# A language-model tower on one core: half of the code-book gates by DRAM, blocks ordered unit first, 8-bit weights rounded in the first stage, projections unrolled in one stage

## The chip, the cores and the metric

One core of one Trainium2 chip runs the whole kernel in one launch. The metric is the device time of that core in microseconds (us). Its engines are TensorE (PE), VectorE (DVE), ScalarE (ACT), GpSimd (POOL) and SyncE (SP), which only issues DMAs here. The profile calls the weight loads of TensorE PEld.

## The reference, cut to what matters

2048 tokens (16 rows of 128) of width 192 pass an embedding and four layers; each layer adds an attention part and a feed-forward part, both behind a layer norm. Changed are the embedding, the norm ahead of the first feed-forward (16 experts, the best 8 of a router), the 8-bit attention of the third layer and its code-book feed-forward.

```python
# embedding
return token_emb + pos_emb[None, :, :] + segment_emb    # segment: rows of a 2-row table
# 8-bit attention, third layer
x_int, s_x = _act_quant(x)            # one scale: the largest |x| of all tokens
wq_int, s_wq = _weight_quant(w_qkv)   # a scale for each output row
acc_s = s_x * s_wq
qkv_int = jnp.einsum('bnc,oc->bno', x_int, wq_int) + _round_ste(b_qkv / acc_s)
qkv_f = qkv_int * acc_s
s_qkv = jnp.maximum(jnp.max(jnp.abs(qkv_f)) / QMAX, EPS)
...
out_int = jnp.einsum('bnc,oc->bno', ctx8, wp_int) + _round_ste(b_proj / out_s)
return out_int * out_s
# code-book feed-forward, third layer: S=8 subspaces, M=64 codes, K=4 kept, R=16, H=32
z = jnp.einsum('nd,sdr->nsr', xf, P)
scores = jnp.einsum('nsr,smr->nsm', z, C)
topv, topi = jax.lax.top_k(scores, K)
w = jax.nn.softmax(topv, axis=-1)
h = jax.nn.gelu(jnp.einsum('nsr,nskrh->nskh', z, W1[sidx, topi]) + b1[sidx, topi])
yl = jnp.einsum('nskh,nskhr->nskr', h, W2[sidx, topi]) + b2[sidx, topi]
comb = jnp.einsum('nskr,nsk->nsr', yl, w).reshape(N, S * R)
out = jax.nn.gelu(comb @ G1 + g1b) @ G2 + g2b
```

## The kernel before, in words

P is 128, D 192 and NB 16: a tile is 128 tokens, and four tiles (GS) make one of four groups (NG) of 512 columns (GT). Each part of the tower is one or more stages; a stage has one program for each engine, tied by semaphores, and ends with all engines at one point. Within a stage an engine takes its instructions in the order in which the code writes them. `Chain` (`c.step`) makes each step of VectorE wait for the one before it.

**First stage**, `embed_stage` (L95). SyncE loads the ids and small tables, GpSimd gathers 16 tiles of rows of the table by indirect DMA into `held_h`, all on one semaphore. VectorE waits for all of them, adds the positions to all 16 tiles in one instruction (L145), and then adds the segment row in 32 instructions (L149).

**Norms**, `norm_stage`. VectorE centres and scales tiles, PE turns them (L289 to L293), ScalarE copies the turned columns out. Only the norm of the first feed-forward has a `wide` output: of its upper 64 columns it wants two copies, in rows 0 to 63 and 64 to 127, so PE multiplies by the identity twice (L293), and one ScalarE copy takes the group. PE runs three groups of turns ahead, then multiplies the first one by the router matrix (L305); ScalarE keeps the logits (L323) and VectorE picks the best 8 (from L387).

**8-bit attention**, `s_l2attn`: the norm n4; `quant_weights_stage` (L2554, tiles `qw_`), which takes the largest |x| (L2611) and lets GpSimd share it over the partitions (L2581), meanwhile rounds the weights, turns them and makes a row of scales, then rounds x and makes the rows (the reciprocal is L2628); `quant_qkv_stage` (L2633, tiles `qq_`), which for each of 16 tiles copies x on GpSimd, turns it on PE, copies it on ScalarE, multiplies, and on VectorE adds the bias (L2700), multiplies by the scale row and takes the maximum; L2709 is the maximum over tiles. Then the heads, and `quant_out_stage` (L2962, tiles `qo_`), with three VectorE instructions a tile (L3048, L3051, L3054) in a loop over pairs of tiles.

**Code-book feed-forward**, `codes_stage` (L1319, tiles `cod_`). All 64 codes of each subspace are computed densely and weighted by gates that are zero but for the best four. A group's work is 32 steps. Step k takes block k % 16 (four codes of 32 hidden units, so 128 rows) of the four subspaces of half k // 16. One subspace of a step is a unit:
- PE: the up matmul into one of three `up` banks (L1459, waits until ScalarE has read what was in the bank), and a matmul of `sel_g` with the turned weights `wt` (L1464), which spreads the gates of the four codes over 128 rows into one of three `gate` banks (waits until VectorE has read what was there);
- ScalarE: gelu with the bias (L1588), into `hp`;
- VectorE: `hp` times the gate bank (L1721).

Behind the four units of step k PE does the down matmuls of step k - 1 (L1480, f32, for the four subspaces side by side) into `comb`; at the first step of each half they are preceded by the b2 bias matmuls (L1475, 24 of them).

Into these steps the order written out in the code puts the preparation of the next group: projection at k = 5, 6; scores at 7 to 10; VectorE's best-4 search at 8 to 11 (L1672, L1686); differences at 9 to 12; spread of z at 12 to 19; marks at 13 to 16; ScalarE's exponential at 15 (L1566); totals and the normed weights at 17 to 21, and their splitting into four bf16 parts `wp` at 19 to 25 (ScalarE's high and mid parts, VectorE's rest and low parts L1710, L1714); and eight turns of `wp` on PE with eight ScalarE copies into `wt` (L1538, 128 x 1024) at 24 to 31. The previous group's output is added at k = 2 to 4. A prologue does the same for the first group, with nothing beside it.

Elsewhere in the tower, and not changed: `b_scratch` in DRAM is read back by broadcast in the second layer (`mam_b_rows`), and the last layer's scatters are GpSimd's indirect DMAs (L1110) beside two VectorE instructions (L1224, L1225).

## Time and profile before

| what | value |
|---|---|
| the runs | 3571.7, 8737.26 and 3560.61 us; median 3571.7 |
| profiled execution | 3563.0 us, its span 3561.2 us |
| mean granted TensorE clock | 0.831 |
| PE busy | 2552.1 us, 72% |
| DVE busy | 2422.7 us, 68% |
| ACT busy | 1601.1 us, 45% |
| POOL busy | 838.6 us, 24% |
| DMA | 114.90 MB, 32 GB/s over the span |
| first stage | to 38.86 us |
| norm and router stage of the first feed-forward | some 236 to 300 us |
| rounding stage, projection stage (8-bit) | 1796.7 to 1823 us, 1824 to some 1871 us |
| output projection (8-bit) | to 2200.9 us |
| code-book stage | norm to 2225, prologue to 2291.2, loop to 2812.2 us |

The busy shares are means over stages that differ: what a stage is worth is read from its own rows. A row of the windows gives each engine's busy time in a stretch; a row of the timeline gives start, duration, engine and line, the tiles out and in, and in brackets how long the engine was idle before it and who ended that. Lines are those of the kernel before.

### The profile page before, as it was taken

What the parts mean: (1) busy time and instruction counts of PE and PEld (TensorE: products, weight loads), DVE (VectorE), ACT (ScalarE), POOL (GpSimd) and SP (SyncE); (2) the same over time, 40 slices, a digit from 0 to 9 for tenths busy, and PEclk for the clock granted to TensorE, in tenths of its full rate; (3) what the DMA queues carried; (4) which work ended last, traced back from release to release, by engine and by line L of the source; (5) the groups of instructions that cost most, each with busy time, mean ns of one, the idle gap of its engine ahead of it and who ended that gap; (6) DMA issues with size and microseconds to landing.
All of it is one profiled execution on the core that took longest, in us unless ns stands there. A gap on an engine that the chain in (4) does not pass through costs nothing. (4 is left out here: it accounts for less than half of the span.)

```text
span 3561.2 us, 39662 instructions
## 1 busy us (share of the span) xinstructions
PE 2552.1 (72%) x13085; PEld 1555.3 (44%) x13132; DVE 2422.7 (68%) x5748; ACT 1601.1 (45%) x2888; POOL 838.6 (24%) x446
## 2 busy tenths in 40 slices
PE   3968995788888876699831112789889777776357
PEld 3955663333434333489721111323222266665335
DVE  4454335399999997211388997687787689999531
ACT  1111112566666652111116772677777545555211
POOL 1000000477676772267300000000000001111022
PEclk9767997799999997799955555899999889887668
DMA  1121001101010100511100000100000100000131
GB/s 37 19 80 45 1 1 31 63 33 70 26 63 33 58 37 0 159 43 40 51 10 1 1 1 1 56 1 1 1 1 1 53 23 1 1 1 1 58 134 54
DMA packets 61429, 114.90 MB, mean 32 GB/s; under 512 B 32685, under 2 KB 50188, under 8 KB 55884
## 3 DMA queue, kind: packets, MB, share of 16 engines
q1 hardware_dynamic: 55084, 100.16, 8.3%
q0 software_dynamic: 6144, 12.25, 1.1%
q8 instruction: 104, 1.70, 0.2%
q14 instruction: 97, 0.79, 0.1%
HBM read 98.31 MB, written 21.99 MB: 34 GB/s over the span
## 5 line engine op out<-in xcount | busy, mean ns | idle before, releaser
L1943 POOL TENSOR_TENSOR mam_st<-mam_du,mam_b_rows 128x1536 f32<-128x1536 f32 x128 | 439.5, 3440 | 172.8 <-PE mam_ysum L2012 172.3
L2173 DVE TENSOR_TENSOR_SCAN mam_st<-mam_da,mam_st 128x512 f32<-128x512 f32 x384 | 441.1, 1204 | 35.9 <-ACT mam_da L2113 18.2
L1721 DVE TENSOR_TENSOR cod_hp<-cod_hp,cod_gate 128x512 f32<-128x512 f32 x512 | 324.0, 681 | 122.2 <-ACT cod_hp L1588 122.0
L2012 PE MATMUL mam_ysum<-mam_st,held_ident 128*128 128x512 f32 x768 | 390.0, 648 | 2.2 <-DVE mam_st L2179 2.2
L1588 ACT ACTIVATE cod_hp<-cod_up,cod_b 128x512 f32<-128x512 f32 x512 | 318.8, 692 | 130.2 <-PE cod_up L1459 129.8
L2113 ACT ACTIVATE mam_da<-mam_delta,mamw_decay 128x508 f32<-128x508 f32 x384 | 254.2, 683 | 184.2 <-DVE mam_st L2173 149.5
L2294 POOL TENSOR_TENSOR att_probs<-att_se,att_neg 128x1536 f32<-128x1536 f32 x16 | 55.0, 3438 | 997.0 <-DVE att_neg L2499 997.0
L2179 DVE TENSOR_TENSOR mam_st<-mam_st,mam_c_ps 128x1536 f32<-128x1536 f32 x128 | 224.4, 1753 | 16.9 <-PE mam_c_ps L2007 13.4
L2012 PEld LDWEIGHTS mam_ysum<-mam_st,held_ident 128*128 128x128 f32 x768 | 159.8, 208 | 167.9 <-issue 160.8
L489 DVE SCALAR_TENSOR_TENSOR held_h<-x_dn,held_gate,held_h 128x192 f32<-128x192 f32 x256 | 89.1, 410 | 183.6 <-PE x_dn L456 181.9
L1464 PE MATMUL cod_gate<-cod_wt,cod_sel_g 128*128 128x512 bf16 x465 | 182.2, 392 | 39.0 <-DVE cod_hp L1721 38.4
L1459 PE MATMUL cod_up<-cod_zr,cod_w1r 96*128 96x512 bf16 x512 | 199.0, 389 | 14.1 <-ACT cod_hp L1588 9.5
L2499 DVE MATCH_REPLACE8 att_neg<-att_top,att_neg 128x128 f32<-128x128 f32 x768 | 201.1, 275 | 0.9 <-issue 0.9
L2492 DVE MAX8 att_top<-att_neg 128x8 f32<-128x128 f32 x768 | 154.8, 277 | 21.3 <-ACT att_neg L2412 14.2
L289 PE MATMUL n_turned<-held_ident,held_xw 128*96 128x128 f32 x224 | 46.2, 390 | 149.8 <-DVE held_xw L254 149.8
L479 ACT ACTIVATE x_ht<-x_up 128x512 f32<-128x512 f32 x96 | 52.1, 595 | 212.6 <-PE x_up L446 212.6
L1927 POOL MEMSET mam_u_pre<- 128x1608 f32 x1 | 1.4, 1437 | 607.6 <-POOLq L73 607.6
L1480 PE MATMUL cod_comb<-cod_hp,cod_w 128*16 128x512 f32 x1024 | 137.1, 608 | 3.0 <-DVE cod_hp L1721 3.0
L456 PEld LDWEIGHTS x_dn<-x1w_w,x_ht 128*128 128x128 f32 x768 | 123.5, 190 | 35.6 <-issue 35.6
L456 PE MATMUL x_dn<-x1w_w,x_ht 128*128 128x192 f32 x768 | 137.4, 333 | 0.0
L790 DVE TENSOR_TENSOR gr_o<-gr_dn,gr_w2c 128x192 f32<-128x192 f32 x40 | 14.3, 358 | 173.1 <-PE gr_dn L671 173.1
L722 ACT ACTIVATE gr_ht<-gr_up 128x512 f32<-128x512 f32 x80 | 39.2, 490 | 205.9 <-PE gr_up L660 205.9
(525 smaller groups left out, 5477.0 us busy)
## 6 DMA issues: line engine op xcount, KB each, us to landing
mam_b_rows<-b_scratch SPq DMA_DIRECT2D x32, 1024.0 KB, 8.0
slot_scratch<-in_slot_fresh SPq DMA_DIRECT2D x2, 3860.0 KB
sw_w<-in_L_w SPq DMA_DIRECT2D x1, 6144.0 KB, 18.6
gr_w<-in_L_w SPq DMA_DIRECT2D x1, 5376.0 KB, 42.2
gr_w<-in_L_w SPq DMA_DIRECT2D x1, 4608.0 KB
sw_w<-in_L_w SPq DMA_DIRECT2D x1, 4608.0 KB, 31.3
gr_rows<-slot_scratch SPq DMA_DIRECT2D x40, 96.5 KB, 1.9
x1w_w<-in_L_w SPq DMA_DIRECT2D x1, 3072.0 KB
```

The costliest lines, as they stand in the source:

```text
L456: last = nc.tensor.matmul(dn[x % 2][:, t, 0:D], ht[(g * NT + f) % NHT][:, t * P:(t + 1) * P], w2_sb[:, f, :], start=(f == first[e]), stop= ...
L1459: nc.tensor.matmul(up[u % BANKS][:], w1r[:, sub, f * P:(f + 1) * P], zr[g % 2][:, sub, :], start=True, stop=True).then_inc(up_ready, 1)
L1464: nc.tensor.matmul(gate[u % BANKS][:], sel_g[:, code, :], wt[g % 2][:, 2 * sub + half, :], start=True, stop=True).then_inc(gate_ready, 1)
L1588: nc.scalar.activation(hp[step % HOLD][:, j, :], up[u % BANKS][:], ACT.Gelu_apprx_tanh, bias=b1[:, sub * HT + f:sub * HT + f + 1]).then_in ...
L1721: nc.vector.tensor_tensor(at, at, gate[u % BANKS][:], ALU.mult).then_inc(gated, 1)
L1943: nc.gpsimd.tensor_tensor(st[it % N_ST][:], du[r % 2][:], along(b_rows[:, p % RING, n % PIECE, :], 1, [P, MC, MT]), ALU.mult)\
L2012: last = nc.tensor.matmul(ysum[:, c, :], m.ident[:], st[it % N_ST][:, c, :], start=False, stop=(it % DS == DS - 1))
L2113: nc.scalar.activation(live(da[:, c, :], r % 2), live(delta[r % 2][:, c, :], r % 2), ACT.Exp, scale=decay[:, c, n:n + 1]).then_inc(exp_rea ...
L2173: nc.vector.tensor_tensor_scan(fs, fa, fs, 0.0, ALU.mult, ALU.add).then_inc(scanned, 1)
L2179: nc.vector.tensor_tensor(x[:], x[:], along(c_ps[:], 1, [P, MC, MT]), ALU.mult).then_inc(weighted, 1)
L2492: last = nc.vector.max(top[:, n, :], cut[:, n, :])
L2499: last = nc.vector.match_replace(rev, top[:, n, :], rev, -BIG)
```

## The change

**Gates.** Of the four subspaces of a half, two (QP = 2) keep their gates from PE; for the other two (QD = 2) PE turns the normed weights themselves in f32 (`turn_gates`, k = 23, 24), ScalarE copies them to `turned_gates`, SyncE stores them to `gate_scratch` in DRAM by four DMAs a group (at k = 28), and for each step brings 512 KB back, broadcast over the hidden units (128 x 4 KB), into a ring of five `wide_gates`. The product of these subspaces reads SBUF. `up` has four banks, `gate` two. `wp` and `wt` hold only half, so that the splits go over 256 columns and four turns (k = 25 to 28) stand for eight. The rows of a block are ordered unit first, code second. The b2 bias of the two subspaces by DRAM is one f32 matmul each.

**8-bit attention.** The weights are rounded, turned and given their row of scales in the first stage, and stored in DRAM; n4 loads them ahead. The two stages become one, unrolled over the 16 tiles: x is rounded in four pieces, three accumulator banks, no GpSimd copies, the maximum is taken over tiles for each column, once a group, and multiplied by the scale row once at the end. The output projection is unrolled, its VectorE instructions take four tiles.

**First stage.** Positions and segments are summed into `base` while the gathers run (16 VectorE instructions, 16 ScalarE scaled copies, one sum), and each group of four tiles is added when its rows are in.

**Norm with `wide`.** One turn in place of two matmuls, and three ScalarE copies for one.

```diff
@@ embed_stage @@
+            sp.wait_ge(q_kept, 2)
+            sp.dma_start(m.q_turned, q_turned[:]).then_inc(q_out, 16)
+            sp.dma_start(m.q_row, q_row[:]).then_inc(q_out, 16)
+            sp.wait_ge(q_out, 32)
...
-            v.wait_ge(rows_in, 16 * NB)
-            c.step(nc.vector.tensor_tensor(m.h[:], m.h[:], along(pos[:], 1, [P, NB, D]), ALU.add))
...
+            c.step(nc.vector.tensor_tensor(base[:], base[:], second[:], ALU.add))
+            for g in range(NG):
+                at = slice(g * GS, (g + 1) * GS)
+                v.wait_ge(rows_in[g], 16 * GS)
+                last = nc.vector.tensor_tensor(m.h[:, at], m.h[:, at], base[:, at], ALU.add)
@@ norm_stage @@
-                        for row in (0, D - P):
-                            last = nc.tensor.matmul(bank[row:row + D - P, 1, at], x[:, P:D], m.ident[:], start=True,
-                                                    stop=True)
+                        last = nc.tensor.transpose(bank[0:D - P, 1, at], x[:, P:D], m.ident[:])
@@ codes_stage @@
-BANKS = 3
+BANKS = 4
+GBANKS = 2
+QP = 2
+GRING = 5
+SEND_AT = 28
...
+            def bring_gates(g, k):
+                step = g * STEPS + k
+                if step >= GRING:
+                    sp.wait_ge(gated, QS * (step - GRING + 1))
+                sp.dma_start(wide_gates[:, step % GRING].rearrange("p j t -> p (j t)"),
+                             along(m.gate_scratch[g % 2, k // HT, k % HT].rearrange("e j t -> e (j t)"), 0,
+                                   [SH, ET, QD * GT])).then_inc(gates_in[step % GRING], 16)
...
+                if j >= QP:
+                    return
+                if u >= QS:
+                    pe.wait_ge(gated, u - QS + 1)
...
+                    for j in range(QD):
+                        rows, at = slice(j * SM, (j + 1) * SM), 32 * (QP + j)
+                        nc.tensor.matmul(comb[at:at + 32, :], b2d[rows, half, :], turned_gates[rows, half, :],
+                                         start=True, stop=False)
...
-                v.wait_ge(gate_ready, u + 1)
-                nc.vector.tensor_tensor(at, at, gate[u % BANKS][:], ALU.mult).then_inc(gated, 1)
+                if j < QP:
+                    v.wait_ge(gate_ready, QP * step + j + 1)
+                    by = gate[j][:]
+                else:
+                    v.wait_ge(gates_in[step % GRING], 16 * (step // GRING + 1))
+                    by = wide_gates[:, step % GRING, j - QP, :]
+                nc.vector.tensor_tensor(at, at, by, ALU.mult).then_inc(gated, 1)
@@ quant_qkv_stage @@
-                    c.step(nc.vector.tensor_tensor(real[k][:], row, z.acc_row[:], ALU.mult))
-                    nc.vector.tensor_reduce(tile_max[:, bass.ds(t, 1)], real[k][:], AX.X, ALU.max,
-                                            apply_absolute_value=True).then_inc(dve2, 1)
+                if t % GS == GS - 1:
+                    g = t // GS
+                    c.step(nc.vector.tensor_reduce(parts[:, g], z.qkv[:, g * GS:t + 1].rearrange("p t n -> p n t"), AX.X,
+                                                   ALU.max, apply_absolute_value=True))
```

## Rows read from the trace of the kernel before

**Rows 1.** Windows, code-book loop: window, length, busy by engine, PEclk, DMA share, GB/s
```profile
2431.20:2570.80 139.60, 124.60 (x673) 40.01 (x684) 108.45 (x260) 103.18 (x167) 0.00 (x0) 0.96 0.00 1
...
2707.70:2812.20 104.50, 97.06 (x543) 28.28 (x550) 78.09 (x126) 76.00 (x127) 0.00 (x0) 1.00 0.00 1
...
2349.60:2353.60 4.00, 3.68 (x19) 1.20 (x19) 4.00 (x21) 3.02 (x7) 0.00 (x0) 1.00 0.00 0
```

**Rows 2.** Timeline, plain step: start, duration, instruction, [idle before, releaser]
```profile
2782.99 0.39 PE L1459 MATMUL cod_up<-cod_zr,cod_w1r 96*128 96x512 bf16 x1
...
2783.21 0.38 PE L1464 MATMUL cod_gate<-cod_wt,cod_sel_g 128*128 128x512 bf16 x1
...
2783.41 2.42 ACT L1588 ACTIVATE cod_hp<-cod_up,cod_b 128x512 f32<-128x512 f32 x4 [0.78 <-PE cod_up L1459]
...
2784.14 2.48 DVE L1721 TENSOR_TENSOR cod_hp<-cod_hp,cod_gate 128x512 f32<-128x512 f32 x4 [0.72 <-ACT cod_hp L1588]
...
2784.88 0.39 PE L1464 MATMUL cod_gate<-cod_wt,cod_sel_g 128*128 128x512 bf16 x1 [0.19 <-DVE cod_hp L1721]
...
2785.20 1.05 PE L1480 MATMUL cod_comb<-cod_hp,cod_w 128*16 128x512 f32 x8
...
2786.18 0.39 PE L1459 MATMUL cod_up<-cod_zr,cod_w1r 96*128 96x512 bf16 x1
```

**Rows 3.** Groups of instructions, code-book loop: busy, mean ns, idle before
```profile
L1538 ACT ACTIVATE cod_wt<-cod_misc 128x1024 bf16<-128x1024 bf16 x24 | 24.8, 1035 | 0.0
...
L1475 PE MATMUL cod_comb<-cod_wt,cod_b_part 128*32 128x512 bf16 x192 | 11.8, 381 | 0.0
...
L1714 DVE TENSOR_TENSOR cod_wp<-cod_ex,cod_wp 128x512 bf16<-128x512 f32 x12 | 8.2, 686 | 0.3 <-ACT cod_wp L1574 0.3
```

**Rows 4.** Timeline of DVE at the exponential of the first group
```profile
2362.70 1.28 DVE L1721 TENSOR_TENSOR cod_hp<-cod_hp,cod_gate 128x512 f32<-128x512 f32 x2 [4.14 <-ACT cod_hp L1588]
```

**Rows 5.** DMA view: GB/s in 40 slices of 200 us; one issue
```profile
GB/s 0 80 423 342 0 0 0 0 0 0 3 0 0 0 0 0 0 0 0 0 0 2 203 421 226 0 0 0 0 0 0 0 0 0 0 0 10 351 429 59
...
gr_w<-in_L_w SPq DMA_DIRECT2D x1, 5376.0 KB, 42.2
```

**Rows 6.** Timeline of the 8-bit projections, both stages
```profile
1796.69 3.35 DVE L2611 TENSOR_REDUCE qw_x_max<-held_xw 128x1 f32<-128x3072 f32 x1 [3.51 <-PEq L73]
...
1804.28 0.38 POOL L2581 PARTITION_ALL_REDUCE qw_x_all<-qw_x_max  x1 [72.60 <-issue]
...
1818.04 3.75 DVE L2628 RECIPROCAL qw_inv_row<-quant_acc_row 128x576 f32<-128x576 f32 x1
...
1863.73 0.75 DVE L2700 TENSOR_TENSOR quant_qkv<-qq_acc,quant_bias_row 128x576 f32 x1
...
1866.30 0.17 DVE L2709 TENSOR_REDUCE qq_all_max<-qq_tile_max 128x1 f32<-128x16 f32 x1
```

**Rows 7.** Timeline of the 8-bit output projection, first and last of 48
```profile
2179.04 0.36 DVE L3048 TENSOR_TENSOR qo_part<-qo_acc,qo_b_int 128x192 f32<-128x192 f32 x1 [0.21 <-DVE qo_b_int L3042]
...
2200.49 0.36 DVE L3054 TENSOR_TENSOR held_h<-held_h,qo_part 128x192 f32 x1 [0.15 <-DVE qo_part L3051]
```

**Rows 8.** Timeline of the first stage, VectorE
```profile
24.46 3.36 DVE L145 TENSOR_TENSOR held_h<-held_h,emb_pos 128x3072 f32<-128x3072 f32 x1 [17.99 <-DMA held_h<-in_table,emb_ids]
...
28.11 10.75 DVE L149 SCALAR_TENSOR_TENSOR held_h<-emb_types,emb_seg_is,held_h 128x192 f32<-128x192 f32 x32
```

**Rows 9.** Timeline of the last stage's scatters
```profile
3405.84 3.36 DVE L1225 TENSOR_TENSOR held_h<-held_h,sw_wide 128x3072 f32<-128x3072 f32 x1
3406.94 3.09 POOL L1110 DMA_INDIRECT slot_scratch<-held_xw,sw_slot_in  x1 [0.30 <-issue]
3410.33 0.96 POOL L1110 DMA_INDIRECT slot_scratch<-held_xw,sw_slot_in  x1 [0.31 <-issue]
```

**Rows 10.** Router stage of the first feed-forward: PE group, then a VectorE row
```profile
L293 PE MATMUL n_turned<-held_ident,held_xw 128*64 128x128 f32 x64 | 11.2, 449 | 0.0
...
271.87 0.29 DVE L387 TENSOR_REDUCE n_top_v<-held_logits 128x8 f32<-128x128 f32 x1 [10.82 <-ACT held_logits L323]
```

More of the change, by code:

```diff
@@ L1418, in spread_z, with turn_gates, turn_w @@
                 last.then_inc(ready, 1)
-            def turn_w(g, i, bank, ready):
-                t, h = i // 2, i % 2
+            def turn_gates(g, half, bank, ready):
+                pe.wait_ge(weighted, GS * (g + 1))
+                for t in range(GS):
+                    at = t * SS + half * QS + QP
+                    last = nc.tensor.transpose(bank[:, t * P:(t + 1) * P],
+                                               ex[:, at:at + QD, :].rearrange("p n e -> p (n e)"), m.ident[:])
+                last.then_inc(ready, 1)
+            def turn_w(g, t, bank, ready):
                 pe.wait_ge(w_low, GS * g + t + 1)
@@ new lines, in products @@
+            def products(t):
+                pe.wait_ge(copied, t + 1)
+                if t >= NACC:
+                    pe.wait_ge(summed, t - NACC + 1)
+                for n in range(2):
+                    for c in range(2):
+                        last = nc.tensor.matmul(acc[t % NACC][:, n, 0:N], xt[t % 2][:, c, :],
+                                                z.wt[:, c, n * N:(n + 1) * N], start=(c == 0), stop=(c == 1))
+                last.then_inc(acc_ready, 1)
+            pe.wait_ge(z.w_in, 48)
```

471 lines of the change are left out of this document (247 added, 224 removed).

## The prediction

> **What bounds the kernel now.** I read the windows first, to find out which of the changed stages are long. The code-book loop (first product to last) fills some 518 us of the 3561.2 us span: 139.6 us for the second group of four tiles, some 137 each for the first and third, 104.5 for the last [rows 1]. No engine is full there: in the second group PE 124.6, DVE 108.5 and ACT 103.2 of 139.6. So I opened the timeline of one step without side work [rows 2]. The reader is to see a ring: up product at 2782.99 (the next matmul 0.22 us later), four gelus from 2783.41, four products from 2784.14, the last gate matmul at 2784.88 (it had to wait for DVE to free one of three banks), then the down products from 2785.20, next step's first up product at 2786.18. Period 3.20 us, while four gelus take 2.31 (2.42 less the last one's tail: 0.58 each), four products 2.40 (0.60 each), and PE would need 8 x 0.22 + 1.0 = 2.8. Nearly all steps of the last group are of this kind. In steps that prepare the next group, DVE is the bound: at 2349.6 to 2353.6 it is busy 4.00 of 4.00 us [rows 1].
>
> **The loop, part by part.** Gates for two of four subspaces leave PE: 4 x 0.22 = 0.9 us a step less. Up banks go from 3 to 4, and a gate bank now waits only for the product one step back, so the ring no longer closes inside one step. What is left in a plain step: PE 6 x 0.22 + 1.0 + 0.1 = 2.4, DVE 2.40, ACT 2.31. The new ring spans two steps: a step's last product, down (0.06 + 0.99), up (0.43), gelu (0.69), four products (2.48), 4.7 us for two, 2.35 for one. I take 2.45, between 2.35 and today's 3.20. The product with the broadcast gate reads two SBUF operands in place of PSUM and one; a 512-column DVE instruction with SBUF operands takes 686 ns [rows 3] against 681, so no change in price. The last group has 27 plain steps and 5 with more (two b2 steps, three with the previous group's output): 27 x 2.45 + 2 x 5.0 + 4.3 + 2 x 3.2 = 87 against 104.5 + 3 for its first turns; gain 20.
>
> In the other groups I take each step as the largest of its three engines' sums and list what it loses. Steps 8 to 19 remain DVE's (products 2.4 plus up to 2.9 of maxima, marks, weights) and lose nothing. Steps 20 to 24: the four rest and four low instructions go over half the columns, 686 ns [rows 3] to about 0.36: 2.6 us. Steps 24 to 28: four turn copies of 1.03 us on ACT instead of eight [rows 3], 3.65 becomes 3.4: 1.4. Steps 29 to 31 become plain: 3.5. Steps 5 and 6 keep 1.9 us of projection on PE: 5.0 becomes 4.3: 1.4. Steps 7, 8 and 12: 1.7. Steps 1 to 4, the previous group's output: 2.1. The exponential stalls DVE for 4.14 us [rows 4]; with four banks ACT can be about one step ahead, so some 2.5 of stall is left, and a slow step less behind it: 3.1. Against that stand two gate copies of 0.58 on ACT and, at both halves, 12 bf16 bias matmuls two abreast instead of 24 four abreast (eight such batches are 11.8 us, 1.48 each [rows 3]; the same number of rounds stays) and two f32 ones (0.6 to 0.9), which the down products queue behind: 2.5. Sum 13.3 for each of three groups, to about 124. The whole loop: 3 x 13.3 + 20 = **60**. Bounds: 25 if plain steps fall only to 2.9 and others not at all, 78 if all overlaps fully.
>
> **The new transfers.** Each step brings 512 KB: 128 descriptors of 4 KB. SyncE issues it when the product five steps before is done, so it has some four steps, 10 us. The nearest row: the Mamba stage's broadcasts from scratch, of the same shape of source (1024 KB each), move 423 and 421 GB/s in full slices of 5 us [rows 5]. At that rate 512 KB is 1.25 us of a 2.45 us step. SyncE has nothing else in this stage but the four stores of the next group's gates at step 28, before the next group's first load, which has four steps of cover. Cost nil; without this cover each microsecond above 2.45 is paid in plain steps.
>
> **The stage's start.** Four wide turn copies of 1.03 [rows 3] fewer, and half of the splitting, less two gate copies: **4**, between 2 and 7. Its first transfer waits for the gate copies, is ready some 7 us later, and the first product that reads it is about 9 us away: hidden.
>
> **Projections.** Before, the weights' rounding and the 16 projections are two stages. From the maximum of x at 1796.69 to the maximum over all tiles at 1866.30 it is 69.6 us [rows 6]. New: x maximum 3.35; then GpSimd's all-reduce, which started at 1804.28 though its input was there at 1800.04 [rows 6]. This 4.2 us lay under the weights' work; now that is gone and DVE waits, to 1804.7 (1804.28 + 0.38). Scale steps 1.2, rounding in four pieces 12 x 0.5 = 6.0 (both estimates by width), rows with the 3.75 us reciprocal [rows 6] 5.6: 1817.5. Then 16 additions of 0.75 [rows 6] (0.82 with their waits) and four maxima over 2304 elements, 2.5 each (3072 elements take 3.35 [rows 6]): 23. Final maximum 2.5 + 0.8 + 0.8. That is 1844.8, where 1866.4 stands: **21**, bounds 14 (PE's matmuls, by an estimate 1.1 us a tile at half clock, become the pace) and 25 (the all-reduce comes at once). The multiply by the scale row and the maximum of each tile go; GpSimd's copies too, none of which ended a wait of DVE.
>
> **Output projection.** 48 small instructions of about 0.36 us, each with a gap behind it [rows 7], run from 2179.04 to 2200.85. New: 12 of 768 columns, 0.95 each: 11.4, after a rounding that four pieces make 0.9 longer: end 2191.0: **10**, bounds 6 and 12.
>
> **First stage.** The position add and 32 type adds, 14.4 us after the last row landed [rows 8], become one add of 3.36 ahead, and four of 0.9 as rows come in. ScalarE's part decides when the base is whole: weights' rounding on DVE ends at 12.5, PE turns and row matmuls to 17.8, copies to 18.7, 16 scaled copies of 0.25 (an estimate, between 0 and a 512-wide copy's 0.58) to 23, base whole at 26.4. SyncE's two stores end before. Now a stall: while DVE ran a 3.36 us instruction with two SBUF operands, a GpSimd indirect transfer took 3.09 us, in place of 0.96 beside an idle DVE [rows 9]. Gathers today run beside an idle DVE; new, DVE has some 13 us of such work then. At the same share the last row lands near 32, the stage's work ends near 33 instead of 38.86: **6**, bounds 2 and 10.
> The Trainium skill, page "SBUF — State Buffer", section "Who interferes with whom", has VectorE and GpSimd share a port pair that is held for a whole instruction; it counts the fast modes of tensor_scalar and copies among those that hold back GpSimd's descriptors, and infers that a tensor_tensor does not. The tensor_tensor of rows 9 does, so the measurement decides here; by the page only some 2 us of DVE's work would count and the term would be 8.
>
> **Router stage of the first feed-forward.** Each tile's two 64-row f32 matmuls are 64 matmul records of 449 ns [rows 10], and become one transpose: PE's turn of four tiles from 4.1 to about 1.9. The gate's first instruction comes at 271.87, 10.82 us late, for logits; the turn and route matmuls ahead of them run without a gap; three turns lie ahead of them: 3 x 2.2 = 6.6, less 0.3 for three ScalarE copies in place of one: **6**, bounds 0 (copies of 0.6 x 3 pace it) and 7.
>
> **Sum.** 60 + 4 + 21 + 10 + 6 + 6 = 107 from the profiled execution's 3563.0 (span 3561.2 and 1.8 around it): 3456. The runs shown are 3560.6 and 3571.7 (a third, 8737, is no measure); I name **3456**.
>
> **Rivals.** (A) PE stays the pace. For: PE is busy 97.06 of 104.5 us of the last group [rows 1] and is in order, with gate, down and bias matmuls in one queue. Then plain steps stay at 2.9, and prepared steps as they are: loop gain 25, time 3491. Against: its own sum is 2.4. (B) Slower than before: the broadcast is the pace. A 5376 KB load landed in 42.2 us, 128 GB/s [rows 5]. At 128 GB/s a step is 4.1 us, today's average, so there the loop gains nothing; the kernel is slower from (512 + 47) / 128 = 4.4 us a transfer on, and at 5.0 it takes 3563 - 47 + 128 = 3644. For: 64 MB are added to 115. Against: the two full slices at 421 to 423, with the same shape of source. (C) Transfers take 3.0 a step: plain steps alone pay, 39 x 0.55 = 21: 3477. (D) The new gates don't ease the loop, since steps 8 to 24 are DVE's and these rule: that is in the sum, and caps it; with plain steps gaining only in the last group the loop gives 35, time 3481.
>
> **Chances.** Forecast 0.66; A 0.12, B 0.05, C 0.07, D 0.10. The range 3415 to 3500 takes in A, C and D; B is left out, and what is better than 78 in the loop. About 2% can be told from no change, 71 us: faster 0.88, same 0.08, slower 0.04.
>
> **What would show it.** Plain steps of the last group at 2.4 to 2.5 us with DVE without gaps; groups near 124; the product's waits on a gates_in DMA at none; 3 us gathers in the first stage beside DVE's instructions; an idle DVE of about 4.5 us ahead of the projection's scale steps; 48 us from the maximum of x to that of all tiles. Wrong if a DMA ends DVE's waits, if steps 25 to 31 stay above 3.5, or if the granted clock in the loop falls below the 0.96 to 1.00 of now [rows 1].

## The result, and the profile after

The changed kernel takes 3469.99 us (median of 4 runs, 3465.39 to 3473.44), the kernel before 3569.11; the ratio is 0.9728, interval 0.9716 to 0.974, without the run of 8737.26 us of the kernel before. The profiled execution took 3465.39 us with a span of 3463.6, 97.6 us less than that of before. Forecast were 3456 us for the kernel and a gain of 107 us. Where the 97.6 us are, each stage from its first VectorE instruction to the next one's in the two timelines:

| stretch | before | after | gained | forecast |
|---|---|---|---|---|
| first stage | 39.9 | 33.0 | 6.8 | 6 |
| norm and retention (same code) | 197.9 | 192.9 | 5.0 | 0 |
| router stage and experts | 362.0 | 351.7 | 10.3 | 6 |
| projections, up to the heads | 75.8 | 63.8 | 12.0 | 21 |
| output projection | 36.3 | 29.2 | 7.1 | 10 |
| norm n5 and prologue, to the first product | 92.3 | 90.8 | 1.5 | 4 |
| code-book loop, first product to next norm | 526.8 | 466.9 | 59.9 | 60 |
| all else (same code, but for what n4 loads) | | | -5.0 | 0 |

These are two single executions. Four profiles whose loop has the code of the changed kernel (this one and three of the experiments) have it at 465.8 to 468.4 us, two with the code of before at 526.8 and 529.1: the 59.9 us are good to some 2 us, and a difference of 1 or 2 us between two profiles says nothing.

The windows of the loop's second and last group, against [rows 1]:

```profile
2376.70:2502.10 125.40, 107.24 (x571) 34.32 (x580) 105.36 (x261) 98.77 (x165) 0.00 (x0) 0.96 0.44 140
2627.20:2712.10 84.90, 81.27 (x467) 22.36 (x472) 75.95 (x127) 75.39 (x127) 0.00 (x0) 1.00 0.52 173
```

139.6 became 125.4 and 104.5 became 84.9. PE lost 17.4 us of busy time in the second group (124.6 to 107.2); the granted clock of these two windows is as before. New is the DMA column: in the last group 0.52 of the engines and 173 GB/s. That is 173 x 84.9 = 14.7 MB, 28 transfers of 524 KB, and 0.52 x 84.9 / 28 = 1.58 us of the DMA engines' time for each, of a step of 2.40. The timeline of two plain steps of the last group and of the first step of its second half, against [rows 2]:

```profile
2668.52 1.28 DVE L1850 TENSOR_TENSOR cod_hp<-cod_hp,cod_gate 128x512 f32<-128x512 f32 x2
...
2668.66 1.05 PE L1596 MATMUL cod_comb<-cod_hp,cod_w 128*16 128x512 f32 x8
...
2669.71 1.29 DVE L1850 TENSOR_TENSOR cod_hp<-cod_hp,cod_wide_gates 128x512 f32<-128x512 f32 x2
...
2670.92 1.28 DVE L1850 TENSOR_TENSOR cod_hp<-cod_hp,cod_gate 128x512 f32<-128x512 f32 x2
...
2671.06 1.05 PE L1596 MATMUL cod_comb<-cod_hp,cod_w 128*16 128x512 f32 x8
...
2673.62 0.60 ACT L1700 ACTIVATE cod_comb_t<-cod_comb 128x512 f32<-128x512 f32 x1
...
2674.27 1.47 PE L1587 MATMUL cod_comb<-cod_wt,cod_b_part 128*32 128x512 bf16 x12 [0.75 <-ACT cod_comb_t L1700]
...
2675.67 1.05 PE L1591 MATMUL cod_comb<-cod_turned_gates,cod_b2d 64*32 64x512 f32 x4
...
2676.65 1.05 PE L1596 MATMUL cod_comb<-cod_hp,cod_w 128*16 128x512 f32 x8
...
2678.78 1.29 DVE L1850 TENSOR_TENSOR cod_hp<-cod_hp,cod_gate 128x512 f32<-128x512 f32 x2 [2.66 <-ACT cod_hp L1708]
```

Down products stand at 2668.66 and 2671.06: a step is 2.40 us, where before it was 3.20. VectorE's products (two by PE's gates at 2668.52, two by the wide gates at 2669.71, then 2670.92) have no bracket, so it never waits: 4 x 0.60 is the step. Further down stands what I had priced too low. From 2673.62 ScalarE copies the sum, PE waits 0.75 us for it, then runs 12 bf16 bias matmuls (1.47), the f32 ones (0.98 to the next start), and only then the down and up products; VectorE is idle for 2.66 us, and from 2671.06 to 2676.65 this step takes 5.59.

The granted clock is not as before in the other groups. The whole loop, before and after, and an up matmul of step 11 of the second group after:

```profile
2294.00:2812.20 518.20, 465.04 (x2552) 146.58 (x2598) 404.54 (x908) 387.06 (x626) 0.00 (x0) 0.98 0.00 1
...
2254.20:2712.10 457.90, 404.01 (x2167) 124.18 (x2206) 392.42 (x908) 372.37 (x620) 0.00 (x0) 0.96 0.46 149
```

```profile
2424.17 0.63 PE L1569 MATMUL cod_up<-cod_zr,cod_w1r 96*128 96x512 bf16 x1
```

By groups it was 0.97, 0.96, 0.99 and 1.00 and is 0.94, 0.96, 0.95 and 1.00. At the lower of the two levels (0.5, 1.2 GHz) such a matmul takes 0.63 us and not 0.38, and step 11 of the second group, which stands in such a stretch, takes 5.84 us, where the first group's takes 4.02 at the full level. Before, this step took 4.01 in all three groups. In the four profiles of the new loop 31 to 38 us of it stood at the lower level, in the two of the old loop 17 and 21 us. TensorE has less to do in the new loop; that this is the reason is not shown.

Who waited for the wide gates, and how long their transfers took, from the view of that tile:

```profile
  ACT cod_hp L1708: 24.7, 34
...
DMA to landing us min/median/max: 3.4/3.9/7.6
```

In the loop VectorE waited for ScalarE before these products, never for a transfer; the slowest landed 7.6 us after its issue.

The projections, against [rows 6]:

```profile
1777.26 3.35 DVE L2748 TENSOR_REDUCE qq_x_max<-held_xw 128x1 f32<-128x3072 f32 x1 [4.37 <-PEq L73]
1783.04 0.38 POOL L2704 PARTITION_ALL_REDUCE qq_x_all<-qq_x_max  x1 [71.66 <-issue]
...
1793.00 3.75 DVE L2757 RECIPROCAL qq_inv_row<-quant_acc_row 128x576 f32<-128x576 f32 x1
...
1798.08 3.47 DVE L2762 TENSOR_TENSOR quant_qkv<-qq_acc,quant_bias_row 128x576 f32<-128x576 f32 x4
...
1801.70 4.20 DVE L2768 TENSOR_REDUCE qq_parts<-quant_qkv 128x576 f32<-128x2304 f32 x1 [0.15 <-DVE quant_qkv L2762]
...
1829.44 4.05 DVE L2770 TENSOR_REDUCE qq_most<-qq_parts 128x576 f32<-128x2304 f32 x1
```

From the maximum of x to the end of the maximum over the tiles (1835.07) it is 57.8 us, not 48. The first addition, at 1798.08, stands 20.8 us after the start as forecast, but by luck: the all-reduce came 1.8 us earlier than forecast (VectorE idle for 2.84 us and not some 4.5), and the rounding in four pieces took 7.8 us instead of 6.0. Behind it each maximum over a group takes 4.20 and the last 4.05, where I had 2.5, and the 16 additions with their gaps take 14.6, where I had 13.1.

The output projection's first and last instruction on VectorE, against [rows 7]:

```profile
2150.04 0.96 DVE L3110 TENSOR_TENSOR qo_work<-qo_acc,qo_b_int 128x768 f32<-128x768 f32 x1
...
2161.04 0.96 DVE L3113 TENSOR_TENSOR held_h<-held_h,qo_work 128x768 f32<-128x768 f32 x1
```

The first stage, against [rows 8]:

```profile
17.26 2.99 POOL L141 DMA_INDIRECT held_h<-in_table,emb_ids  x1 [0.31 <-issue]
...
19.25 5.62 ACT L179 ACTIVATE emb_second<-emb_types,emb_seg_is 128x192 f32<-128x192 f32 x16
...
24.98 3.36 DVE L207 TENSOR_TENSOR emb_base<-emb_base,emb_second 128x3072 f32<-128x3072 f32 x1 [5.55 <-ACT emb_second L179]
25.56 3.60 POOL L141 DMA_INDIRECT held_h<-in_table,emb_ids  x1 [0.30 <-issue]
```

VectorE waits for ScalarE's 16 scaled copies, 0.35 us each, then sums the base. One gather beside VectorE's instructions took 2.99 us and one 3.60.

The router stage, against [rows 10]: a group, then VectorE's first instruction of the gate.

```profile
L353 PE MATMUL n_turned<-held_ident,held_xw 128*64 128x128 f32 x16 | 6.1, 389 | 0.0
```

```profile
250.53 0.29 DVE L450 TENSOR_REDUCE n_top_v<-held_logits 128x8 f32<-128x128 f32 x1 [2.72 <-ACT held_logits L382]
```

The 64 records of 449 ns are 16 of 389, and the wait of 10.82 us is 2.72. The first 16 route matmuls of the stage, 258.71 in the timeline of before and 242.38 in that of after:

```profile
258.71 4.37 PE L305 MATMUL n_route_ps<-n_wr,x1w_wide 128*128 128x16 f32 x16
```

```profile
242.38 2.66 PE L364 MATMUL n_route_ps<-n_wr,x1w_wide 128*128 128x16 f32 x16
```

The granted clock also differs by chance. The retention stage between the first norm and the second has the same code in both kernels. Its window before, after, and in the second experiment below, which has the same code up to there as the changed kernel:

```profile
70.83:237.71 166.88, 149.65 (x1208) 137.93 (x1208) 77.05 (x167) 27.48 (x95) 0.00 (x0) 0.77 0.13 20
```

```profile
63.07:225.91 162.84, 146.43 (x1208) 134.91 (x1208) 77.20 (x166) 27.37 (x95) 0.00 (x0) 0.79 0.13 20
```

```profile
64.17:233.03 168.86, 152.41 (x1208) 140.21 (x1208) 77.18 (x166) 27.43 (x95) 0.00 (x0) 0.76 0.13 20
```

With 0.77, 0.79 and 0.76 granted it took 166.9, 162.8 and 168.9 us. Over all executions profiled here this stretch lay between 162.8 and 169.5 us, so its 4.0 of the 5.0 us in the table are no gain of the change. The other stretches moved 5.0 us the other way together, none by much more than 2, so the two cancel and the sum stands on the changed stages.

### The profile page after: what moved, and what is told of

It is laid out like the page before. It is cut to its first block and busy times, and to the rows that moved or that the text cites. A ratio compares the mean times of both kernels' runs of the same rounds, so it can differ in the third digit from the quotient of the medians.

```text
span 3463.6 us, 38446 instructions
## 1 busy us (share of the span) xinstructions
PE 2484.2 (72%) x12628; PEld 1541.3 (44%) x12668; DVE 2402.1 (69%) x5684; ACT 1594.3 (46%) x2912; POOL 830.5 (24%) x414
## 5 line engine op out<-in xcount | busy, mean ns | idle before, releaser
L1850 DVE TENSOR_TENSOR cod_hp<-cod_hp,cod_gate 128x512 f32<-128x512 f32 x256 | 163.5, 679 | 46.5 <-ACT cod_hp L1708 45.9
L1569 PE MATMUL cod_up<-cod_zr,cod_w1r 96*128 96x512 bf16 x512 | 180.1, 390 | 15.6 <-ACT cod_hp L1708 9.4
L1850 DVE TENSOR_TENSOR cod_hp<-cod_hp,cod_wide_gates 128x512 f32<-128x512 f32 x256 | 164.8, 685 | 24.8 <-ACT cod_hp L1708 24.7
L853 DVE TENSOR_TENSOR gr_o<-gr_dn,gr_w2c 128x192 f32<-128x192 f32 x40 | 14.3, 358 | 172.9 <-PE gr_dn L734 172.9
```

The lines of the kernel that those rows point to most:

```text
L1569: nc.tensor.matmul(up[u % BANKS][:], w1r[:, sub, f * P:(f + 1) * P], zr[g % 2][:, sub, :], start=True, stop=True).then_inc(up_ready, 1)
L1850: nc.vector.tensor_tensor(at, at, by, ALU.mult).then_inc(gated, 1)
```

## The experiments

**One half of the change each.** The first kernel is that of before with the code-book stage's edits alone (its constants, its units, the order of the rows of its weights), the second is the changed kernel with the code-book stage of before.

> The kernel before with the code-book part of the change alone. If the parts add up, as the sum of the prediction has it, this stage gives what the traces of before and after show between its first VectorE instruction and the next norm: 586.4 - 523.3 = 63 us, so about 3563 - 63 + 1 = 3501 us, ratio 0.982 to 0.984. Rival: the transfers or the clock couple it to its neighbours, then the sum with the other half of the change misses 98 us by more than 5.

Measured: 3504.26 us, ratio 0.9827 (0.9811 to 0.9843). The loop took 465.8 us, as in the changed kernel (466.9).

> The changed kernel with the code-book stage of before. If the parts add up: 98 - 62 = 36 us less than before, about 3527 us, ratio 0.988 to 0.992. Of it 7 us from the first stage, 8 to 10 from the router stage, 12 from the projections, 7 from the output projection; the retention stage between the first and second norm, whose code is the same, was 4 us shorter at a granted clock of 0.79 for 0.77: if that comes of the earlier start it is here again, and if it is chance of one execution it is gone.

Measured: 3531.84 us, ratio 0.9905 (0.9888 to 0.9921). 1.73% and 0.95% make 2.68%, and both together gave 2.72%: the halves add up. Each half alone gains less than 2%, and neither interval reaches a ratio of 1. The retention stage was 168.9 us here, so its 4 us were chance.

**Four up banks and two gate banks, all gates by TensorE.**

```diff
-BANKS = 3
+BANKS = 4
+GBANKS = 2
@@
-                if u >= BANKS:
-                    pe.wait_ge(gated, u - BANKS + 1)
+                if u >= GBANKS:
+                    pe.wait_ge(gated, u - GBANKS + 1)
...
-                nc.tensor.matmul(gate[u % BANKS][:], ...
+                nc.tensor.matmul(gate[u % GBANKS][:], ...
```

> The kernel before with four up banks and two gate banks, all gates still by TensorE. Theory: the fourth up bank alone does not open the ring, since the last gate matmul of a step now waits for the product two units back and the down products queue behind it: product, gate 0.22, down 1.0, up 0.43, gelu 0.69, two products 1.2 make 3.5 us for a plain step, so some 10 to 15 us slower than before. Rival: the banks were the gain and the DRAM gates carry little; then plain steps fall to 2.8 to 2.9 us, TensorE's own sum, and the kernel is 25 to 40 us faster.

Measured: 3630.26 us, plain steps 3.79 us. A plain step in its timeline:

```profile
2830.62 0.39 PE L1465 MATMUL cod_gate<-cod_wt,cod_sel_g 128*128 128x512 bf16 x1 [0.63 <-DVE cod_hp L1722]
...
2831.22 0.39 PE L1465 MATMUL cod_gate<-cod_wt,cod_sel_g 128*128 128x512 bf16 x1
...
2831.53 1.05 PE L1481 MATMUL cod_comb<-cod_hp,cod_w 128*16 128x512 f32 x8
...
2832.52 0.39 PE L1460 MATMUL cod_up<-cod_zr,cod_w1r 96*128 96x512 bf16 x1
```

The third gate matmul, at 2830.62, waits 0.63 us for VectorE to give a gate bank back; behind it in TensorE's order stand the fourth up product, the fourth gate (2831.22, its weights 0.48 us late for the same reason), the down products (2831.53) and the next step's first up product (2832.52, 3.79 behind the one of 2828.73). The theory's direction holds and its size was too small: the kernel (a single run) is 64 us slower and the loop 66, where 10 to 15 were expected; plain steps came to 3.79 and not 3.5, and steps with side work lengthened as well. The fourth up bank, bought with a gate bank, is a loss without gates by DRAM: what opens the ring is that two of four units ask nothing of TensorE between their up product and the down products.

**Three up banks in the changed kernel** (`BANKS = 3`, nothing else).

> The changed kernel with three up banks in place of four. Theory of the prediction (the fourth bank lets the ring span two steps): plain steps of the last group go from 2.40 to 2.7 to 2.9 us, the loop is 20 to 40 us longer. Rival: with half of the gates gone TensorE is early enough that three banks do, plain steps stay at 2.40, and only the steps around the exponential are up to 2 us longer each, under 8 us in all.

Measured: 3476.81 us; the loop 471.0 us for 466.9. Down products of two consecutive steps:

```profile
2689.84 1.05 PE L1596 MATMUL cod_comb<-cod_hp,cod_w 128*16 128x512 f32 x8
...
2692.31 1.05 PE L1596 MATMUL cod_comb<-cod_hp,cod_w 128*16 128x512 f32 x8
```

2.47 us a step for 2.40, so the rival was nearly right (it had 2.40 and under 8 us in all): the fourth bank is worth 4 us by this one run, 3 to 5 by the spread of the other loops, and the prediction's "up banks go from 3 to 4" was not what the gain needed. (The rest of this execution's surplus lies in the second layer, 782.2 us for 774.0 with the same code, at a granted clock of 0.90 for 0.92.)

**The transfers.** First a ring of four with a second, unread load of the same 512 KB in each step, then a ring of three.

```diff
+                if step:
+                    sp.wait_ge(shadow_in, 16 * step)
+                sp.dma_start(wide_gates[:, 4], ...).then_inc(shadow_in, 16)
                 sp.dma_start(wide_gates[:, step % USED], ...).then_inc(gates_in[step % USED], 16)
```

> The changed kernel with a ring of four slots in place of five, and each step's 512 KB brought twice, once into the fifth slot that nobody reads; so 128 MB pass in the loop in place of 64. Theory (transfers are hidden, at up to 420 GB/s one takes 1.25 us): a step's 1 MB takes 2.5 to 2.9 us, so the 38 or so plain steps become the transfer's, 2.40 to 2.6 to 2.9, loop 8 to 25 us longer, and steps of 3.1 us and more stay as they are. Rival B of the prediction (the rate is 128 to 147 GB/s): 7 to 8 us a step, loop over 900 us.

Measured: 3551.29 us, the loop 543.9 us, 77 more. The group of the products by wide gates, then the DMA view of 60 us in the last group:

```profile
L1857 DVE TENSOR_TENSOR cod_hp<-cod_hp,cod_wide_gates 128x512 f32<-128x512 f32 x256 | 165.5, 690 | 115.4 <-DMA cod_wide_gates<-gate_scratch 91.4 <-ACT cod_hp L1715 24.0
```

```profile
GB/s 292 303 126 298 284 46 19 262 404 77 374 279 150 399 172 363 303 167 393 175 320 350 87 418 210 229 218 251 194 352 153 243 431 71 385 273 202 429 137 330
DMA packets 4179, 15.26 MB, mean 254 GB/s; under 512 B 460, under 2 KB 460, under 8 KB 4176
...
q1 hardware_dynamic: 4176, 15.22, 75.0%
```

SyncE's own waits in the same stretch:

```profile
SPq L1477 <- DMA cod_wide_gates<-gate_scratch: 39.9, 14, 5.5
```

VectorE's idle time before these products is now put down to the transfer (91.4 us), and plain steps are 3.9 us, where 2.5 to 2.9 were expected. But the DMA engines are busy for 75.0% of this stretch only, not full. The queue moved 15.22 MB, 29 transfers of 524 KB, so one takes 0.75 x 60 / 29 = 1.55 us of their time, as in the changed kernel (1.58). Two make 3.1 of the 3.9 us. The rest is a wait that the experiment itself brought: SyncE holds each load back until the unread one of the step before has landed, for 39.9 of these 60 us, and one takes 4.5 us in the median from issue to landing. What it bounds is this: 1049 KB every 3.9 us arrive at least, so a transfer needs no more than 1.95 us of a step of 2.40. Rival B's 128 GB/s is out; the 421 GB/s of [rows 5], by which I had 1.25 us, is 0.3 us short of what the shares show. But single slices of 1.5 us moved 399 to 431 GB/s here as well, so the share counts time in which the engines were busy below that rate, and it is no proof that a transfer alone cannot pass in 1.25 us.

> The changed kernel with three slots of broadcast gates in use in place of five. The transfers landed 3.4 to 7.6 us after their issue, 3.9 in the median. With three slots a transfer is issued when the product three steps back is done, so it has two steps, 4.8 us in plain ones, less the issue. Theory: plain steps stay at 2.4 and the loop within 3 us, with single waits of VectorE for a transfer. Rival: what counts is the slowest transfer (7.6 us): waits in many steps, loop 10 to 40 us longer.

Measured: 3472.68 us, the loop 467.6 us, every plain step 2.40. Its tile view:

```profile
  ACT cod_hp L1709: 24.8, 34
...
  DMA cod_wide_gates<-gate_scratch: 0.2, 1
...
DMA to landing us min/median/max: 3.5/3.9/5.5
```

One wait of 0.2 us in 128 steps. Three slots do, and 8 KB a partition could be had back.

**The b2 bias.** Left out, moved, and moved to better places.

```diff
                 if k % HT == 0:
                     pe.wait_ge(comb_kept, step // HT)
-                    for q in range(2 * NPART):
...
-                    for j in range(QD):
...
+                    for j in range(QS):
+                        nc.tensor.matmul(comb[32 * j:32 * j + 32, :], blank[:], wt[g % 2][:, 0, :],
+                                         start=True, stop=False)
...
+                for q in B2_AT.get(k, ()):
...
+                if k in B2D_AT:
...
```

The first loop holds the 12 bf16 bias matmuls and the second the two f32 ones. Where they are left out, four bf16 matmuls with zeros open the accumulation and the output lacks b2; where they are moved, the new ones stand behind the down products of step k.

> The changed kernel without the b2 bias matmuls (12 bf16 and 2 f32 ones at the first step of each half); four bf16 matmuls with zeros open the accumulation in their place, so the output lacks b2. Theory: the two down steps that carry them are 5.6 us where plain ones are 2.4, and 2.4 of the 3.2 us are these matmuls, on TensorE, ahead of the down products, with nothing beside them: the step falls to some 3.4 us, and 8 of them give 8 x 2.2 = 18 us (13 to 20) in the stage. Rival: what stretches these steps is ScalarE's copy of the sum behind its gelus, which the matmuls wait for: then at most 6 us.

Measured: 3454.93 us, the loop 450.7 for 466.9: 16.2 less, where 18 (13 to 20) were expected. The theory holds.

> The changed kernel with the b2 bias matmuls taken from the first step of each half and put behind the down products of steps 8 to 10 and 17 to 19 (bf16) and 13, 14, 20, 21 (f32), where VectorE is the bound in the first three groups; four bf16 matmuls with zeros open the accumulation. Theory: TensorE has 1 to 2 us to spare in those steps, so the first three groups keep the 2.2 us of each of six steps, and the last group, whose steps are all at VectorE's and TensorE's 2.4, gets back only the drained pipeline, 1 us each: 6 x 2.2 + 2 = 15 us less than the changed kernel (10 to 18), about 3454 us. Rival: TensorE's order delays the next up products whatever VectorE does, and the time only moves: within 4 us of the changed kernel.

Measured: 3464.55 us, ratio 0.9713 (0.9695 to 0.973); the loop 461.9.

> As the kernel with the b2 matmuls moved, with the places taken from its steps: there the f32 pairs behind step 14 and 21 cost 0.9 and 0.8 us, those behind 13 and 20 nothing, the bf16 ones behind 8 and 17 0.4 each, and the last group lost 6 us for 4 gained. Now bf16 behind 7, 8, 10 and 19, 20, f32 behind 9, 13, 18, 20, and in the last group at the head of each half as in the changed kernel. Theory: six steps give 2.16 us each, and the rest costs under 0.5 us a group: 11 to 13 us less than the changed kernel in the stage (523.3 to about 511). Rival: any matmul put into a step delays its up products and so VectorE, because ScalarE is only one step ahead: then 6 us or less.

Measured: 3458.12 us, ratio 0.9685 (0.9669 to 0.97); the loop 457.3. The length of single steps of the second group (us): the distance from the start of the down products of the step before to that of their own, so that a matmul put behind the down products of step k falls in step k + 1 of the table:

| step | changed | left out | moved | placed |
|---|---|---|---|---|
| 0 | 5.60 | 3.44 | 3.45 | 3.44 |
| 9, 10 | 3.42, 5.35 | 3.41, 5.35 | 3.77, 5.00 | 3.77, 4.99 |
| 15 | 6.49 | 6.48 | 7.37 | 7.37 |
| 16 | 7.77 | 5.61 | 5.16 | 5.30 |
| 22 | 3.07 | 3.07 | 3.84 | 3.07 |
| 0 and 16 of the last group | 5.60, 5.60 | 3.44, 3.44 | 3.44, 3.45 | 5.60, 5.59 |
| 15 of the last group | 2.40 | 2.40 | 3.36 | 2.40 |

The bias costs 2.16 us at each of eight steps (5.60 less 3.44), the remaining 1.0 is the wait for ScalarE's copy (0.75 in the rows of the changed kernel above) and the four matmuls with zeros. What moves is free where VectorE has more than its products (steps 9 to 11 together, 19 to 21), costs 0.4 in step 18 of the first of the two, and costs its full 0.9 or so for an f32 one in two kinds of step: plain ones, and step 15, whose exponential stands behind two gelus in ScalarE's order, so that whatever delays the up products of that step delays the exponential. The theory held in sign for both moves and was too large: 5.0 us and 9.6 us in the loop, where 15 and 12 were expected.

**The maxima of the projections.** ScalarE writes absolute values, VectorE takes contiguous elementwise maxima.

```diff
-                    c.step(nc.vector.tensor_reduce(parts[:, g], z.qkv[:, g * GS:t + 1].rearrange("p t n -> p n t"), AX.X,
-                                                   ALU.max, apply_absolute_value=True))
+                    c.step(nc.vector.tensor_tensor(parts[:], size[g % 2][:], parts[:], ALU.max))
```

> The changed kernel with the projections' maxima taken otherwise: ScalarE writes the absolute values of each finished tile, VectorE takes an elementwise maximum over four tiles at once (three for the 16 tiles), then over 2 and 1 tiles. The four reductions that read with a stride took 4.19 us each and the last 4.05, where the prediction had 2.5: 20.8 us. Theory: the stride is the price; contiguous maxima of 2304 elements take 2.45, so 3 x 2.45 + 1.25 + 0.7 = 9.3 and up to 2 us of waits for TensorE or ScalarE: 9 to 11 us less between the maximum of x and that of all tiles (57.8 to about 48), about 3459 us for the kernel. Rival: TensorE's tile (1.17 us) is next: 16 x 1.17 = 18.7 instead of 31.4, so at most as much as that and never under 45 us.

Measured: 3459.49 us, ratio 0.9693 (0.9678 to 0.9707). The stretch from the maximum of x (1782.15) to that of all tiles:

```profile
1813.66 2.56 DVE L2777 TENSOR_TENSOR qq_parts<-qq_size 128x2304 f32<-128x2304 f32 x1
...
1818.56 0.76 DVE L2783 TENSOR_TENSOR quant_qkv<-qq_acc,quant_bias_row 128x576 f32<-128x576 f32 x1 [1.43 <-PE qq_acc L2727]
...
1829.98 0.75 DVE L2795 TENSOR_REDUCE qq_all_max<-qq_most 128x1 f32<-128x576 f32 x1
```

48.6 us for 57.8: 9.2 less, as the theory has it. The same 2304 elements take 2.56 us side by side and took 4.20 with a stride. The run changes the instruction too (an elementwise maximum in place of a reduction, with the absolute value on ScalarE), so the stride is not taken alone. Two rivals are unlikely by rows: the last maximum has the stride without the absolute value and took 4.05, and reductions of 512 elements side by side took 0.69 us with 8 elements for each output (L443) and 0.67 with 64 (L1823), so that many short runs cost nothing to speak of there. At 1818.56 VectorE now waits for TensorE's products (1.43), the rival's limit, but only for three tiles.

**Two earlier starts.** ScalarE's scaled copies ahead of its other copies in the first stage; the 2 MB of w1 loaded in the norm ahead of the code-book stage.

```diff
-    norm_stage(nc, m, a, "n5")
+        norm_stage(nc, m, a, "n5", ahead=((w1, "S_w1", w1_in),))
```

> The changed kernel with two loads or copies earlier. First stage: ScalarE's 16 scaled copies before its copies of the turned weights and the row, so that they start at 14.1 in place of 19.25 and the base is whole at some 23.5 in place of 28.3. Theory: then the last gather, which lands some 2 us behind its issue, rules: the stage ends near 29 in place of 31.9, 2 to 4 us less. Rival: a gather beside the base sum stretches to 3.6 us and those behind it are pushed, so nothing is gained. Code-book stage: the 2 MB of w1 are loaded in the norm ahead; VectorE waited 15.4 us for them and TensorE 10.95 us for VectorE's splitting. Theory: 9 to 12 us less between the norm and the first product. Rival: the other loads of the stage, 3 MB, then end the wait: 3 us or less.

Measured: 3465.04 us, ratio 0.9704 (0.9688 to 0.9721). The norm and prologue took 82.9 us for 90.8, 7.9 less, where 9 to 12 were expected; the first stage gained nothing (33.4 us for 33.0). Its rows:

```profile
19.83 3.36 DVE L207 TENSOR_TENSOR emb_base<-emb_base,emb_second 128x3072 f32<-128x3072 f32 x1 [0.33 <-ACT emb_second L172]
20.63 3.38 POOL L141 DMA_INDIRECT held_h<-in_table,emb_ids  x1 [0.30 <-issue]
...
31.36 0.96 DVE L211 TENSOR_TENSOR held_h<-held_h,emb_base 128x768 f32<-128x768 f32 x1 [4.11 <-DMA held_h<-in_table,emb_ids]
```

The base is summed 5.15 us earlier, but the gather beside it takes 3.38 us, and the last addition waits 4.11 us for rows: the rival was right. And the first rows of the code-book stage:

```profile
2194.43 3.51 POOL L1487 MEMSET cod_wp<- 128x4096 bf16 x1 [48.40 <-POOLq L73]
2194.47 5.62 DVE L1857 CAST cod_hp<-codw_wide_gates 128x4096 bf16<-128x4096 f32 x1 [4.43 <-PEq L73]
```

VectorE's cast of w1 took 5.62 us, where it took 2.29 in the changed kernel, because it now meets GpSimd's 3.51 us memset: that began at 2194.43 and ended at 2197.94, and 2.15 us later, about the cast's own 2.29, the cast is done (2200.09). GpSimd's next memset, from 2197.99, took 2.55 us beside it, where it took 0.52 in the changed kernel.

**All of these in one kernel.**

> The three last kernels in one. Different stages and nothing shared but the queue of loads, so the gains add: 10 + 12 + 3 + 10 = 35 us less than the changed kernel, about 3433 us (3425 to 3445), ratio to the kernel before 0.960 to 0.966.

Measured: 3446.09 us (median of 5), ratio 0.9653 (0.9637 to 0.9669) to the kernel before, the best of all. In its profile the projections took 54.9 us (63.8), norm and prologue 81.5 (90.8), the loop 458.3 (466.9): 26.8 us of gains where 35 were expected; the first stage gave none, the b2 places less. The median is 23.9 us below that of the changed kernel and just above the expected range of 3425 to 3445.

## Why the prediction was right, and where not, point by point

- **The loop (60, measured 59.9).** The total is right, and its core as well: plain steps 2.40 for 2.45, DVE without gaps, transfers hidden. The four groups gained 14.3, 14.2, 11.8 and 19.6 for 13.3 three times and 20; in the third, which gained least, the granted clock fell most, from 0.99 to 0.95. The second group by steps, as the distances between the starts of their down products in the two timelines (us):

| steps of the second group | before | after | gained | forecast |
|---|---|---|---|---|
| 0, 15 and 16 (bias, exponential) | 19.9 | 19.9 | 0.0 | 0.6 |
| 1 to 4 (previous output) | 17.9 | 15.8 | 2.1 | 2.1 |
| 5 to 14 | 43.0 | 40.8 | 2.2 | 3.1 |
| 17 to 19 | 12.6 | 11.0 | 1.7 | 0 |
| 20 to 24 (half-width rest) | 21.0 | 17.7 | 3.3 | 2.6 |
| 25 to 28 (turns) | 14.7 | 13.0 | 1.7 | 1.4 |
| 29 to 31 (plain) | 10.6 | 7.2 | 3.4 | 3.5 |

  Several terms were off and cancelled, so that the total is nearer than its parts. "Steps 8 to 19 ... lose nothing" was wrong for 17 to 19: 17 fell from 3.85 to 3.07 and 18 from 4.40 to 3.48. VectorE's sum did not bind step 17 before, since VectorE sat idle in it:

```profile
2512.72 1.28 DVE L1721 TENSOR_TENSOR cod_hp<-cod_hp,cod_gate 128x512 f32<-128x512 f32 x2 [0.94 <-ACT cod_hp L1588]
```

  It waited for the gelus, and these for up products that stood behind the down products and the spread of z. The exponential's step was priced at 3.1 us of gain and gave 1.9 (8.39 to 6.49), though the stall itself came to 2.44 us for the 2.5 forecast; ScalarE's exponential there is 1.91 us between two table loads of 1.28 each. A step with the bias was priced at 5.0 us in the last group and took 5.60; in the second group step 0 lost 1.1 (4.52 to 5.60) and step 16 lost 0.8 (6.97 to 7.77). In steps 5 to 14 the first group gained 3.3, as forecast, and the second 2.2, since its step 11 ran at the lower clock. The granted clock of the loop was given as a sign, and by groups it did fall below 0.96; the forecast had no term for it.
- **Which edit did it.** "Up banks go from 3 to 4" was given as part of the reason; three up banks give 2.47, so this is some 4 us of the 60. That gates leave TensorE is the step that counts: with all gates there and the same four banks a plain step is 3.79.
- **The transfers (nil).** Right: no wait in the loop, with 1.58 us of the engines' time a transfer where I had 1.25, and at most 1.95. Of the five slots three do; how much bandwidth is spare is known only between these bounds.
- **Stage start (4, measured 1.5).** From VectorE's first split to the first product 3.1 us were gained; the load of w1 that starts the split came 1.6 us later behind the norm. VectorE waited 15.4 us for it, and I had not looked at what this stage's start waits for. One pair of profiles is thin here: norm and prologue took 88.5 to 91.3 us in the nine profiles with the new code of this stage and 91.7 to 93.3 in the three with the old, 2.5 us apart in the mean.
- **Projections (21, measured 12.0).** The step that failed: "four maxima over 2304 elements, 2.5 each (3072 elements take 3.35)" and the final 2.5. The row I took the price from reads side by side; these read with a stride of 576 elements, 4.20 and 4.05. (4 x 1.7) + 1.55 = 8.4 of the missing 9, the additions were 1.5 longer than I had them, and the contiguous version gives 9.2 back. That the stage began as forecast was two errors of 1.8 us that cancelled, the all-reduce and the rounding. It fell below my lower bound of 14, since I bounded TensorE's pace and the all-reduce but not this price.
- **Output projection (10, measured 7.1).** The twelve instructions run from 2150.04 to 2162.00, 12.0 for 11.4 (and for 21.8 before). What comes before them grew by 2.1 (13.7 to 15.8) where I had 0.9 for the rounding in four pieces (the price that is too low in the projections as well), and 0.6 were added behind them: 9.8 - 2.1 - 0.6 = 7.1.
- **First stage (6, measured 6.8).** Right sum, and the gathers do stall; but they did not set the end. ScalarE's copies did (0.35 each, an estimate of 0.25), and only once these were moved did the gathers rule, at the same end.
- **Router stage (6 in the sum, 7 at most; measured 9.5 in the norm, 10.3 with the experts).** The wait fell by 8.1 us. TensorE's first 16 route matmuls took 4.37 us before and 2.66 after; from the norm's start to the gate's first instruction the granted clock was 0.50 before and 0.57 after. It is no chance of one execution: they took 2.66 to 2.69 us in all eleven profiles with the new norm, at the full clock level, and 4.37 in all three with the old. That part I had not in the sum, and it takes the gain above my bound of 7.
- **Rivals.** A and D would have left 25 to 35 in the loop, and 59.9 came. C (3.0 us a transfer) and B (4.4) fall by the doubled loads, 1.95 us at most. B's 3644 us put the loop at 512 us, where the prediction itself has 518: with that it is 3638.

## What to carry to other kernels

Count a step as a ring of waits, not only as sums of engines: the gain here came from the two units that ask nothing of TensorE, not from the added bank, and moving work within such a step is free only where another engine has more to do and where no long instruction queues behind it. Take the price of an instruction from a row with the same access pattern: the same maximum cost 4.20 us with a stride and 2.56 without. Look at the granted clock of each part of a loop after taking work from TensorE: here a step of 4.02 us became 5.84 at the lower level. And judge a hidden transfer by the DMA share of the very window, divided by the transfers in it, beside the peak rate of another stage: the two bound its price from above and below; whoever doubles a load to test it must see that the second load's own wait doesn't become what is measured.

## What the runs showed of the hardware

- A broadcast of 512 KB in 4 KB rows from DRAM over 128 partitions took 1.55 to 1.58 us of the 16 DMA engines' time by their mean busy share (524 KB / 1.58 = 332 GB/s), while the same shape of source moved 421 to 423 GB/s in [rows 5], and single slices of 1.5 us of the doubled loads moved 399 to 431. What the difference is made of is not shown. 254 GB/s were moved in a stretch in which the engines were busy for 75%.
- A VectorE reduction of 2304 f32 elements with a stride of 576 took 4.20 us, 1.82 ns an element; 3072 side by side took 3.35, 1.09 each [rows 6], and the elementwise maximum of 2304 took 2.56, 1.11 each. The Trainium skill ("SBUF — State Buffer", section "Door 1: The DMA port swizzle (why [64,N] ≈ [32,N])", its note on cachelines) says that accesses within one 16-byte line run at full bandwidth and that each that crosses to a new line pays a penalty. The runs are in line with it: here every f32 element is in another line, and it costs 0.7 ns more.
- VectorE's 2.29 us cast took 5.62 us where it started 0.04 us after a 3.51 us GpSimd memset, and ended 2.15 us after the memset did: it waited for nearly the whole of it. The Trainium skill ("SBUF — State Buffer", section "Who interferes with whom") has this: the port pair is held by one engine for a whole instruction.
- GpSimd's gathers, mostly 0.95 us, took 2.99 to 3.60 beside VectorE's two-operand instructions, though some beside the same kind took 1.0 to 1.1. The Trainium skill, in the same section, infers that a tensor_tensor does not hold them back, and here as in [rows 9] the measurement differs.
- Removing matmuls from TensorE's queue went with a lower granted clock in the loop (0.98 to 0.96), and at the lower level a 512-column up matmul took 0.63 us for 0.38.
- The same code at the same place got a granted clock of 0.76 to 0.79 in different executions, 162.8 to 169.5 us of one stage: 6.7 us between two profiles can be that alone.
